# A first feed-forward whose loads and constant rows are issued by other queues, with the first batch's gather, update and table products two slots earlier

## The reference

```python
x = x + 0.5 * _L0_ffn_ref(_layernorm(x), ...)      # first feed-forward: the change is here
x = x + _L0_attn_ref(_layernorm(x), ...)           # attention with relative positions
x = x + 0.5 * _L0_ffn_ref(_layernorm(x), ...)      # the same feed-forward again
x = x + 0.5 * _L1_ffn_ref(_layernorm(x), ...)
x = x + _L1_attn_ref(_layernorm(x), ...)
x = x + 0.5 * _L1_ffn_ref(_layernorm(x), ...)

def _L0_ffn_ref(x, switch_w, switch_b, w1, b1, w2, b2):     # 8 experts, hidden size 512
    route_prob = softmax(t @ switch_w + switch_b)
    routes = argmax(route_prob)
    for e in range(8):
        y = gelu(t @ w1[e] + b1[e]) @ w2[e] + b2[e]
        out = where(routes == e, y, out)
    return out * max(route_prob)
```

## Time and profile before

| | us |
|---|---|
| median of 3 runs | 755.23 |
| the runs | 750.75, 755.23, 757.09 |
| span of the profiled execution | 752.3 |

### The profile page before, as it was taken

One profiled execution on the slowest core, in us unless ns is written; L12 is line 12 of the kernel. 1 busy time (PEld: TensorE's weight loads), 2 busy tenths in 40 slices (PEclk: granted clock), 3 DMA queues, 4 the chain that ended last, 5 costly groups with the idle time before them and its releaser, 6 DMA issues. The chain is left out here.

```text
span 752.3 us, 17249 instructions
## 1 busy us (share of the span) xinstructions
PE 581.5 (77%) x5361; PEld 417.1 (55%) x5361; DVE 532.0 (71%) x1881; ACT 453.5 (60%) x983; POOL 203.6 (27%) x262
## 2 busy tenths in 40 slices
PE   4399993079999999999899998452996673678780
PEld 3288883045666666767576766341985342346450
DVE  7543320967787788999799995873224799867897
ACT  3245562047888888999799996550552534376723
POOL 1745332401912720660400000043443200211200
PEclk9999998589999999999999999655998787799985
DMA  8878567699899999999744421833554000000001
GB/s 241 221 240 289 181 215 205 212 300 331 242 349 330 296 313 309 255 251 345 185 136 141 134 65 22 238 86 127 170 180 121 2 1 0 0 1 1 1 1 56
DMA packets 130378, 127.80 MB, mean 170 GB/s; under 512 B 27962, under 2 KB 108002, under 8 KB 129394
## 3 DMA queue, kind: packets, MB, share of 16 engines
q1 hardware_dynamic: 122722, 99.85, 46.7%
q0 software_dynamic: 3920, 25.26, 8.8%
q10 hardware_dynamic: 3648, 1.59, 0.8%
HBM read 68.37 MB, written 48.79 MB: 156 GB/s over the span
## 5 line engine op out<-in xcount | busy, mean ns | idle before, releaser
L1714 DVE CUSTOM_DVE_ANT_0 l0am_prob<-l0am_ps_s,l0am_bias 128x512 f32<-128x512 f32 x256 | 166.6, 689 | 33.8 <-PE l0am_ps_s L1788 24.1
L1631 ACT ACTIVATE l0am_prob<-l0am_prob,l0am_neg_top 128x512 f32<-128x512 f32 x256 | 171.4, 723 | 6.8 <-DVE l0am_neg_top L1714 6.8
L1801 PE MATMUL l0am_ps_t<-c_ident,l0am_prob 128*128 128x128 f32 x1024 | 129.0, 275 | 0.4 <-DVE l0am_probT L1701 0.4
L1801 PEld LDWEIGHTS l0am_ps_t<-c_ident,l0am_prob 128*128 128x128 f32 x1024 | 110.9, 141 | 16.5 <-issue 8.0
L636 ACT ACTIVATE l0f_h<-l0f_psU,l0f_experts 128x128 f32<-128x128 f32 x212 | 60.7, 369 | 83.0 <-PE l0f_psU L962 82.9
L829 DVE COPY l0f_xsT<-l0f_psT 128x128 f32<-128x128 f32 x53 | 15.4, 291 | 99.0 <-PE l0f_psT L952 99.0
L1701 DVE COPY l0am_probT<-l0am_ps_t 128x512 f32<-128x512 f32 x128 | 82.2, 684 | 1.4 <-PE l0am_ps_t L1801 1.4
L1788 PE MATMUL l0am_ps_s<-l0am_ks,l0am_qs 32*128 32x512 f32 x512 | 74.4, 651 | 3.5 <-DVE l0am_neg_top L1714 2.6
L1625 ACT COPY l0am_probT<-l0am_ps_t 128x512 f32<-128x512 f32 x128 | 68.5, 589 | 10.7 <-PE l0am_ps_t L1801 10.7
L531 POOL DMA_INDIRECT token_results<-l0f_ys,l0f_token_i x53 | 51.1, 965 | 78.3 <-DVE l0f_ys L839 75.0
L1815 PE MATMUL l0am_ps_cg<-l0am_probT,l0am_v 128*9 128x128 f32 x2048 | 68.7, 275 | 2.7 <-DVE l0a_heads L1725 2.7
(11 more groups left out here) (340 smaller groups left out, 949.6 us busy)
## 6 DMA issues: line engine op xcount, KB each, us to landing
l0am_bias<-near_terms SPq DMA_DIRECT2D x128, 192.0 KB, 4.6
near_terms<-l0am_near POOLq DMA_DIRECT2D x6, 3072.0 KB, 12.3
l0f_mine<-l0f_experts SPq DMA_DIRECT2D x53, 256.0 KB, 2.4
near_terms<-l0am_near SPq DMA_DIRECT2D x4, 1536.0 KB, 7.5
l0o_rows_k<-position_k SPq DMA_DIRECT2D x12, 512.0 KB, 6.9
l0f_experts<-in_L_ffn_w SPq DMA_DIRECT2D x2, 2048.0 KB
l0f_experts<-in_L_ffn_w SPq DMA_DIRECT2D x16, 256.0 KB
position_q<-l0o_rows SPq DMA_DIRECT2D x16, 256.0 KB, 4.3
```

The costliest lines, as they stand in the source:

```text
L1631: nc.scalar.activation(prob[:, k, :], prob[:, k, :], ACT.Exp, bias=neg_top[:, k:k + 1], scale=-1.0)\
L1714: dve.tensor_tensor_reduce(out=prob[:, k, :], in0=ps_s[:, j, :], in1=bias[:, j, at:at + S], scale=-1.0, scalar=HUGE, op0=ALU.add, op1=ALU.min,
L1801: last = pe.transpose(ps_t[:, BANK_OF[j], i, :], prob[:, u % SLOTS_, i * P:(i + 1) * P], ident[:, :])
```

## The change

It touches `ffn_phase` alone and has these parts.

- The eight loads of w2 of the first feed-forward are issued by POOL, before its scatters. w1 and w2 get semaphores of their own. SP begins with slot 0 when w1 is in and the slot table is there, without waiting for b2, w2 or b1's copy. PE waits for b1, b2 and w2.
- Of the first part's eight stores of blanks, SP issues four, before slot 0, and ACT the other four.
- The second part's eight stores of blanks are issued by SP, one in each of slots 2 to 9, as plain stores behind a register load. POOL's indirect DMAs for them are gone.
- The gather of batch 0 stands in slot 10 instead of 11, behind slot 10's scatter; update, turn and products stand two slots earlier (15, 18 and 19 to 28), and SP stores products from slot 22 on instead of 24.

In the second feed-forward SP issues what it did before; only its wait in front of slot 0 is for w1 instead of for all the weights and b1's copy.

```diff
+        EARLY_BLANKS = 4 if opening else 0
+        LATER_BLANKS = range(2, 2 + EXPERTS)
-        EXTEND_SLOTS, GATHER_SLOT, UPDATE_SLOT = (11, 13, 15), STARTS[1], STARTS[1] + 6
+        EXTEND_SLOTS, GATHER_SLOT, UPDATE_SLOT = (11, 13, 15), STARTS[1] - 1, STARTS[1] + 4
...
+        def load_down_weights(queue):
+
+            for e in range(EXPERTS):
+                queue.dma_start(experts[:, e, SLAB_W2:SLAB_B2].rearrange("p (k d) -> p k d", k=FC),
+                                w["w2"][e].rearrange("(k p) d -> p k d", p=P)).then_inc(down_weights_in, 16)
+
+        def store_blank(queue, part, e, stored):
+
+            end = queue.value_load(blank_i[0:1, part, e:e + 1], min_val=0, max_val=XS_ROWS - P)
+            queue.dma_start(xs_dram[bass.ds(end, P), :], c["blank"][:, e, 0:XS_COLS]).then_inc(stored, 16)
...
             def _(sp):
-                for dst, src in loads:
-                    sp.dma_start(dst, src).then_inc(weights_in, 16)
-                for e in range(EXPERTS):
-                    sp.dma_start(experts[:, e, SLAB_W2:SLAB_B2].rearrange("p (k d) -> p k d", k=FC),
-                                 w["w2"][e].rearrange("(k p) d -> p k d", p=P)).then_inc(weights_in, 16)
+                sp.dma_start(b1[:, :], w["b1"].rearrange("e (k p) -> (e k) p", p=P)).then_inc(weights_in, 16)
+                sp.dma_start(experts[:, :, SLAB_W1:SLAB_W2], w["w1"].rearrange("e d f -> d e f")).then_inc(up_weights_in, 16)
+                sp.dma_start(experts[:, :, SLAB_B2:SLAB_B1], w["b2"].unsqueeze(0).partition_broadcast(P)).then_inc(weights_in, 16)
+                if not opening:
+                    load_down_weights(sp)
                 if aside:
                     aside.load(sp)
...
-                sp.wait_ge(weights_in, FFN_LOADS * 16)
-                sp.wait_ge(b1_ready, 1)
+                if opening:
+                    sp.wait_ge(blanks_ready, 1)
+                    for e in range(EARLY_BLANKS):
+                        store_blank(sp, 0, e, blanked[e])
+                sp.wait_ge(up_weights_in, 16)
                 sp.wait_ge(rows_ready, 1)
...
                         row = packed_of(sp, s + AHEAD)
+                        if opening and s in LATER_BLANKS:
+                            if s == LATER_BLANKS[0]:
+                                sp.wait_ge(blanks_ready, 2)
+                            e = LATER_BLANKS.index(s)
+                            store_blank(sp, 1, e, later_blanked[e])
                         load_mine(s + AHEAD, row)
                         load_tokens(s + AHEAD, row)
...
             def _(pool):
                 pool.wait_ge(ids_set, 1)
+                if opening:
+                    load_down_weights(pool)
...
-                    if opening and s < EXPERTS:
-                        if s == 0:
-                            pool.wait_ge(blanks_ready, 2)
-                        pool.indirect_dma_start(
-                            xs_dram[:, :], bass.IndirectOffsetOnAxis(ap=blank_i[:, 1, s:s + 1], axis=0),
-                            c["blank"][:, s, 0:XS_COLS], None).then_inc(later_blanked[s], 16)
...
-                for e in range(EXPERTS):
-                    end = act.value_load(blank_i[0:1, 0, e:e + 1], min_val=0, max_val=XS_ROWS - P)
-                    act.dma_start(xs_dram[bass.ds(end, P), :], c["blank"][:, e, 0:XS_COLS]).then_inc(blanked[e], 16)
+                for e in range(EARLY_BLANKS, EXPERTS):
+                    store_blank(act, 0, e, blanked[e])
...
-                pe.wait_ge(weights_in, FFN_LOADS * 16)
+                pe.wait_ge(weights_in, 2 * 16)
+                pe.wait_ge(down_weights_in, EXPERTS * 16)
```

More of the change, by code:

```diff
@@ L36 @@
 YS_ROWS = TILES * P + 2 * EXPERTS * P
-FFN_LOADS = 3 + EXPERTS
 SLAB_W1, SLAB_W2 = 0, FF
@@ L400, in ps_rank @@
             return psU[:, g % 2, 0, 0:5 * EXPERTS].rearrange("p (t e) -> p t e", t=5)
-        weights_in = sem("weights_in")
+        weights_in, up_weights_in = sem("weights_in"), sem("up_weights_in")
+        down_weights_in = soft_dma_sem("down_weights_in")
         chain = sem("chain")
@@ L411, in ffn_phase @@
         blanked = [sem(f"blanked{e}") for e in range(EXPERTS)]
-        later_blanked = [soft_dma_sem(f"later_blanked{e}") for e in range(EXPERTS)] if opening else []
+        later_blanked = [sem(f"later_blanked{e}") for e in range(EXPERTS)] if opening else []
         b1_psum, b1_ready = sem("b1_psum"), sem("b1_ready")
```

## The result

| | before | after |
|---|---|---|
| median, us | 753.13 (7 runs, 750.75 to 757.09) | 760.12 (7 runs, 758.61 to 764.79) |
| span of the profiled execution, us | 752.3 | 757.7 |
| start of the next stage on DVE, us | 131.51 | 139.35 |

The ratio is 1.0100, with a 95% interval of 1.0069 to 1.0131: slower by 1.0%. The interval lies clear of no change, and it reaches to both sides of the 1% that the prediction took as its limit. With four more runs the median of before came to 753.13, 2.1 us under the one that the forecast was built on.

A forecast was written before the change was run, and what follows sets the result against it. It took SP's issue queue in the first feed-forward as the bound; -5.4 + 10.4 - 0.4 = +4.6 us (the first-part blanks 0) on the 755.2 median gave 759.8 us, range 754.5 to 764.5.

The forecast's parts named there:

- Part 3: Second part's eight blank stores on SP in slots 2 to 9: 1.3 us each, +10.4 us, ends +9.2 and +11.6.
- Rival B: Blanks on SP hidden or well under 1.15 us each, front's gain not hidden: -5.4 to 0 us, 750 to 755; chance 0.12.
- Part 1: Phase front, w2 on POOL and narrower wait: SP's first slot 0 copy at 26.4, -5.4 us, ends -6.0 and -4.0.
- I let the small loads end near 20 to 21 and the four blanks, at 1.2 each, near 25.5: SP's queue behind b2, before slot 0: assumed end times of the eight small loads and four blank stores.
- the forecast's window of 25.8 to 27.5: Sign at the front: SP's first copy of slot 0's w1 would start at 25.8 to 27.5 in the changed profile.
- rival C: Front: late w1 or SP's full queue eats the gain; 765.2 us, 1.3% slower, if the delay reaches 6; chance 0.12.
- Part 2: First part's blanks split between ACT and SP: ACT free near 33 instead of 37.2, hidden under SP's 10 us; 0 us.
- Part 4: Gather behind slot 10, update and products two slots earlier: only SP's 0.4 us of waiting goes, -0.4 us.
- The bound: First feed-forward ends when SP's issues are through; PE, POOL or DVE time is worth nothing until exceeding 10 us.
- Rival A: Products, via PE and ACT, set the phase's end: front's gain and two slots arrive, 10.9 us, 744.3; chance 0.08.

The follow-up runs named there:

- e1: The kernel before with only the second part's eight blank stores moved from POOL to SP, in slots 2 to 9; ratio to before 1.0103.
- e2: The changed kernel with the second part's blank stores given back to POOL, the rest as changed; ratio to before 1.0006.
- e9: The kernel before with only w2's loads on POOL and the narrower waits; ACT issues all eight early blanks; ratio to before 0.9981.
- e4: The changed kernel with the attention's eight small loads issued ahead of w1 instead of behind b2; ratio to before 1.0056.
- e8: The changed kernel with small loads ahead of w1, later blanks and last 12 row loads on ACT, old slots; ratio to before 0.9967.
- e12: The changed kernel with small loads ahead of w1, later blanks on POOL, plus ten tiny POOL transfers in slots 15 to 24; ratio to before 0.9969.
- e3: The kernel before with only the slot numbers of gather, update, turn and products changed to those of the changed kernel; ratio to before 1.0007.
- e6: The kernel before with the last 12 of 32 row loads issued by ACT behind its last product, not SP; ratio to before 0.9980.

## Why the prediction was right and where it was wrong

**The verdict** (within 1%, slower side, 759.8 against 760.12) came out, and the mechanism that carries it, Part 3, was right. But the number agreed partly by luck: the sum said +4.6 us, the medians differ by 7.0 and the next stage by 7.84. That error of 2.4 us was cancelled by the base: three runs of before had put it 2.1 us too high. With the terms as measured the sum is -1.8 + 10.3 - 0.4 = +8.1, near the 7.84 of the stage; on the prediction's base that is 763.3, past its own 1%. And "no change that can be measured" was wrong: the interval excludes it.

**Part 3, blanks on SP: +10.4, measured +10.3.** The xs load of slot 13 moved by 70.68 - 62.22 = 8.46 us, and the first mine copy by -1.81; the difference, 10.27, is 1.28 us for each of eight stores. e1 alone gives 10.7. e2 against after gives 8.65 (108.05 against 99.40), and 9.7 without the 1.0 us that SP waits for a product in e2. Rival B falls.

**Part 1, the front: -5.4, measured -1.8, and -0.7 if all profiles of either front are taken** (30.00 and 31.00 against a mean of 31.19). This is the term that was mis-sized. The step that failed is "I let the small loads end near 20 to 21 and the four blanks, at 1.2 each, near 25.5". The small loads ended at 24.35 and the blanks at 29.09. The prediction had seen that a full queue holds SP up and had allowed for it: the eight small loads take 4.4 us without it (22.14 to 26.54 in before), so that letting them run from 7.9 to 20 or 21 allows 8 to 9 us (an estimate). With w2 on POOL it was more: the first issue behind b2 took 12.80 us, 14.10 in e2 and 14.15 in e9, where a small load takes 0.4 to 0.8 without it, and seven small loads and the four blanks still stood behind it. Undoing this one step (e4) brought the first copy to 27.07, inside the forecast's window of 25.8 to 27.5.

So rival C, to which the prediction gave 0.12, came true in good part. By its own count, from the best case of 25.8, the delay was 30.00 - 25.8 = 4.2 us, past the 3.6 at which it calls the kernel over 1% slower. Both of its halves were there. "SP's full queue" set the start in after. And w1 was late: it landed 18.5 us after its issue at 6.24, at 24.7, where the prediction had 23.3 as its worst case (a count that leaves out the 512 KB of b2). By the packet records w1's last packet ended at 17.1 in before and at 24.1 in after. In after SP came to w1 later still and didn't wait; in the kernels with the small loads first w1's landing set the start. These rows are from after, the view of w1's issue; the smaller landing time is that of the second feed-forward, where SP issues w2 behind w1:

```profile
L460 SPq DMA_DIRECT2D l0f_experts<-in_L_ffn_w x2: 420/420/420, 6.2 to 472.7; - x2
DMA to landing us min/median/max: 8.5/13.5/18.5
```

On the rule of the Trainium skill (DMA: Bandwidth & Descriptors, Issuing engines are not separate DMA queues) the trace agrees: the weights landed no sooner, and w1 landed later, beside w2. With w2 on POOL the sixteen engines show a share of 1.10 and 1.03 in the stretches of the earlier trace rows:

```profile
6.00:16.00 10.00, 5.90 (x29) 4.97 (x29) 8.29 (x49) 3.42 (x12) 5.51 (x8) 1.00 1.10 274
16.00:27.00 11.00, 7.39 (x39) 5.34 (x35) 8.73 (x52) 4.51 (x12) 7.51 (x8) 1.00 1.03 312
```

**Part 2, nothing: right.** ACT issues its four blanks in 3.53 us, and nobody gains. PE's first slot came at 36.20, not 34: it waited 7.08 us for tokens, not for b1.

**Part 4, -0.4: right in size on SP, whose 0.4 us of waiting is gone.** What stood behind the moved work was as the prediction had it: the gather is held up in POOL's queue, and DVE waits for its data.

```profile
79.11 0.80 POOL L1229 DMA_DIRECT2D l0a_heads<-token_results  x1 [3.17 <-issue]
80.22 0.98 POOL L549 DMA_INDIRECT token_results<-l0f_ys,l0f_token_i  x1 [0.30 <-issue]
...
83.98 1.14 DVE L1236 SCALAR_TENSOR_TENSOR x_tokens<-l0a_heads,l0o_half_gate,x_tokens 128x128 f32<-128x128 f32 x4 [2.96 <-DMA l0a_heads<-token_results]
```

**The bound.** "A microsecond put on SP there is a microsecond of the kernel" held (after, e1, e4). "Or taken from it" failed beyond 1.6 us: "PE's last group ends 10 us before SP" measured the wrong end of that chain. Behind PE come DVE's addition, the scatter, its landing and POOL's close, 129.04 in all. For this change it made no difference, since SP got longer. In e8 SP ends 11.7 us earlier than before, and the stage starts 1.4 us earlier. Rival A's 744.3 would have needed both chains to end 10.9 us earlier.

**From the phase to the whole.** The stage starts 7.84 us later, the span is 5.4 longer. The other 2.5 us lie between DVE's 129th and 256th scores of the attention: 134.96 us in the profile of before and 131.6 to 133.2 in after and nine of the other profiles (134.5 in e12, 136.8 in e9). In before a stretch shows TensorE at its lower level (0.52 granted), behind 8.9 us at 1.00 in which PE was busy for 6.82. The columns are those of the earlier trace rows; the first row is before, the second a like stretch of after.

```profile
363.90:367.40 3.50, 3.49 (x40) 1.71 (x40) 2.31 (x6) 1.80 (x4) 3.50 (x2) 0.52 1.06 217
```

```profile
371.00:374.50 3.50, 3.42 (x46) 2.21 (x36) 3.45 (x11) 2.38 (x5) 3.50 (x2) 1.00 1.03 221
```

PE is busy for 3.49 us of that stretch; at the upper level the same work would have taken some 1.8, so it can account for 1.7 of the 2.5 us (an estimate from this row). None of the kernels touches the attention, so I take this for a trait of that execution; with one profile of before it isn't shown. A span of one profile can be off by some 2 us for such reasons.

## What to carry to other kernels

Where a queue of issues is the bound, count what it issues: eight small stores with computed addresses cost 10 us there and nothing on POOL, as long as POOL's chain had its 1.6 us to spare. A long issue in a row behind a large transfer is not the cost of that row; ask what comes to stand there once it is moved. Small loads issued ahead of the large one brought SP's start forward by 2.9 us here (e4). And a load moved to another queue goes on competing with those that it has left: w1 landed 7 us later. And before calling an engine 10 us early, follow its chain to the end: results, scatter, landing, and the engine's own close of the phase.

## What the runs showed of the hardware

- Behind w1 (2 MB) and b2 (512 KB) SP's next issue took 5.7 to 6.7 us where SP issued w2 itself (before, e1, e3, e6), and 12.80 to 14.15 us, for a load of 64 KB, where POOL issued w2 at the same time (after, e2, e9). The eight small loads ahead of w1 took 0.4 to 0.6 us each (e4).
- w1's last packet ended at 17.1 us in before and at 24.1 in after, though after had issued it 0.6 us earlier (at 6.24, not at 6.80).
- POOL closes a phase in 3.24, 3.90, 4.55, 5.20 and 6.02 us after 39, 47, 55, 63 and 73 transfers issued by it: 0.08 us each. SP, with 127 issues in the phase before, closes in 0.37 us.
- POOL's issue of eight loads of 256 KB took 6.24 us, 0.8 each, and they landed with a median of 10.4 us. SP needed 13.63 behind w1, of which 5.79 were the first, and 0.77 to 0.84 for four of the last five.
- Where ACT issued loads of rows while POOL's last scatters were under way, POOL's close began 5.5 and 5.6 us behind the start of the last scatter (e6, e8), in the other profiles 2.9 to 4.1. The cause is open.
